# Four-layer residual kernel on one core: four buffers of lags with their folded half built on the core, x1 loaded ahead of the adapter stack, and weights laid out by the host

## The reference

```python
x = x + _L0_cond_ref(x, itok_B_8_3872, ...)   # long convolution per channel
x = x + _L1_cond_ref(x, itok_B_0_15, ...)     # 64x64 channel mix, chosen per sample
x = x + _L2_cond_ref(x, itok_B_6_15, ...)     # x W2^T + bias + rank-16 adapter, chosen per sample
x = x + _L3_cond_ref(x, itok_B_0_2, ...)      # x W3^T + rank-32 adapter, chosen per sample
```

## Time and profile before

| | us |
|---|---|
| median of three runs | 1584.57 |
| the profiled execution | 1583.27 |
| its span, first to last instruction | 1581.1 |
| PE busy | 1487.6 (94%) |
| DVE busy | 1073.5 (68%) |
| ACT busy | 635.6 (40%) |
| POOL busy | 116.0 (7%) |

### The profile page before, as it was taken

The page is one execution under the profiler, slowest core; times in us unless marked ns, Lnnn a source line. Parts: engine busy times, 40 slices in busy tenths (PEclk is TensorE's granted clock), DMA queues, the critical chain, the costliest instruction groups (busy, mean ns, idle before and its releaser), DMA issues.

```text
span 1581.1 us, 33465 instructions
## 1 busy us (share of the span) xinstructions
PE 1487.6 (94%) x10701; PEld 1422.1 (90%) x10701; DVE 1073.5 (68%) x2203; ACT 635.6 (40%) x1185; POOL 116.0 (7%) x197
## 2 busy tenths in 40 slices
PE   6999999999999996999999999999999999999998
PEld 5888888999989895999999999999999999999988
DVE  7955376676766674676676776677677677677674
ACT  3331256565666652243243243233243233333332
POOL 3551210000000000000000000000000000000000
PEclk9999999999999996999999999999999999999999
DMA  9724289899999986345445445545545545545642
GB/s 244 108 103 114 46 254 294 280 291 298 291 292 286 295 255 209 126 147 178 154 146 180 153 145 174 160 127 185 163 126 186 153 138 162 177 139 159 180 140 74
DMA packets 183699, 289.73 MB, mean 183 GB/s; under 512 B 64065, under 2 KB 120781, under 8 KB 181009
## 3 DMA queue, kind: packets, MB, share of 16 engines
q1 hardware_dynamic: 173436, 254.72, 53.8%
q10 hardware_dynamic: 10230, 34.59, 6.4%
HBM read 214.09 MB, written 75.15 MB: 183 GB/s over the span
## 4 chain that ended last, share of the span: by engine, by line
PE 34%; DMA 9%; SPq 9%; issue 6%; DVE 4%; DVEq 0%; ACT 0%
PE ps L1554 11%; PE ps L1555 11%; DMA x_in<-x_d 8%; PE ps L1525 6%; SPq L1223 5%; SPq L1222 3%; DVE late L1385 2%; PE ps L1564 2%; PE ps L1562 2%; PE ps L1536 1%; PE ps L1531 1%; DVE hrow L1444 1%; DVE hrow L1440 1%; DMA x_nat<-in_x 0%; DVE x_in L1390 0%
## 5 line engine op out<-in xcount | busy, mean ns | idle before, releaser
L1554 PE MATMUL ps<-weights,xs 128*128 128x256 f32 x1536 | 397.4, 289 | 0.0
L1555 PE MATMUL ps<-weights,xs 128*128 128x256 f32 (+1 forms) x1536 | 388.9, 292 | 0.0
L1554 PE MATMUL ps<-weights,xa 128*128 128x352 f32 (+1 forms) x1152 | 331.5, 315 | 4.4 <-DVE weights L1416 1.3
L1555 PE MATMUL ps<-weights,xa 128*128 128x256 f32 (+1 forms) x1152 | 325.5, 297 | 0.0
L1554 PEld LDWEIGHTS ps<-weights,xs 128*128 128x128 f32 x1536 | 292.6, 190 | 0.0
L1555 PEld LDWEIGHTS ps<-weights,xs 128*128 128x128 f32 x1536 | 292.5, 190 | 0.0
L1304 ACT ACTIVATE a<-ps 128x512 f32<-128x512 f32 x128 | 76.6, 599 | 396.6 <-PE ps L1525 396.6
L1554 PEld LDWEIGHTS ps<-weights,xa 128*128 128x128 f32 x1152 | 220.6, 192 | 9.6 <-issue 9.6
L1097 PE MATMUL ps<-toep,ut 128*128 128x512 f32 (+2 forms) x1152 | 227.6, 342 | 0.0
L1555 PEld LDWEIGHTS ps<-weights,xa 128*128 128x128 f32 x1152 | 219.2, 190 | 0.0
L1097 PEld LDWEIGHTS ps<-toep,ut 128*128 128x128 f32 x1152 | 195.0, 189 | 16.8
(11 more groups left out here) (221 smaller groups left out, 2095.6 us busy)
## 6 DMA issues: line engine op xcount, KB each, us to landing
xt<-in_xt SPq DMA_DIRECT2D x64, 512.0 KB, 6.8
x_d<-yo SPq DMA_DIRECT2D x64, 512.0 KB, 4.0
x_in<-x_d SPq DMA_DIRECT2D x64, 512.0 KB, 4.8
x_nat<-in_x SPq DMA_DIRECT2D x64, 512.0 KB, 3.9
out<-y_out ACTq DMA_DIRECT2D x64, 512.0 KB, 4.3
toep_raw<-kern_d SPq DMA_DIRECT2D x64, 384.0 KB, 5.0
toep_raw<-fold_d SPq DMA_DIRECT2D x64, 320.0 KB, 6.3
stack<-b_d SPq DMA_DIRECT2D x130, 128.0 KB, 3.6
```

Source lines behind the costliest of these rows:

```text
L1554: mm(left[0], x_part, left[1], start=first and is_wide, stop=end, skip_group_check=True)
L1555: ins = mm(right[0], x_part, right[1], start=first and is_wide and H_AT[m] > 0, stop=end, skip_group_check=True)
```

## The change

The change has four parts.

1. **Lags.** SP loads one piece of 1024 lags a channel (`lags`, four buffers) instead of 768 plain and 640 folded ones (two buffers). The folded part is no longer made once for all channels in DRAM: DVE adds it up in each channel from `lags` into `fold` (`sums`), two channels ahead, together with the difference of quarters. `fold_in`, `fold_sum` and `fold_d` are gone. `toep` is then rounded in two instructions on ACT and two on DVE instead of one each. `ut` is rounded for seven of its eight blocks (`SPLIT`). The block `tri` is copied behind `dt`, not before it. `yo` has two buffers instead of four, and `lags` and `xt` are both loaded three channels ahead. Before the loop SP waits until the last adapter rows are stored.
2. **Order of loads in a pair.** `load_stack` for pair n moves from the end of round n-1 to round n, behind the loads of `x1_in` for n+1. It reads its adapter numbers again (four `TENSOR_LOAD` more a round).
3. **Mask.** `late` has 16-bit elements and half the columns; its halves and tiles now share one buffer, so a mask waits for the copy before it (`chosen`).
4. **Layout by the host.** W2, W3 and the adapter factors arrive so that what a partition loads is one run in DRAM; 25 loads of factors become 4.

The diff, cut to its core:

```diff
 
             def load_p2(to, i, landed):
-                cols = slice(i * P, (i + 1) * P)
-                sp.dma_start(to[:], w2.rearrange("(c p) t -> p c t", p=P)[:, :, cols]).then_inc(landed, 16)
+                sp.dma_start(to[:], w2[i]).then_inc(landed, 16)
...
-                sp.dma_start(a3raw[:, c, :].rearrange("p (l r) -> p l r", r=R3),
-                             lora3_a.rearrange("l (c p) r -> c p l r", p=P)[c]).then_inc(in_a3, 16)
-            b2_in = lora2_b.rearrange("a (c p) r -> c p a r", p=P)
-            split = 3 * P // R2
-            for c in range(K8):
-                sp.dma_start(b2raw[:, c, :].rearrange("p (a r) -> p a r", r=R2), b2_in[c, :, 0:split]).then_inc(in_b2, 16)
-            for c in range(K8):
-                sp.dma_start(b2raw3[:, c, :].rearrange("p (a r) -> p a r", r=R2), b2_in[c, :, split:A2N]).then_inc(in_b2_3, 16)
-            sp.dma_start(b3_raw[:], lora3_b.rearrange("(c p) r -> p c r", p=P)).then_inc(in_b3, 16)
+            sp.dma_start(a3raw[:], lora3_a).then_inc(in_a3, 16)
+            sp.dma_start(b2raw[:], lora2_b[:, :, 0:3 * P]).then_inc(in_b2, 16)
+            sp.dma_start(b2raw3[:], lora2_b[:, :, 3 * P:AR]).then_inc(in_b2_3, 16)
+            sp.dma_start(b3_raw[:], lora3_b).then_inc(in_b3, 16)
...
 
-            def load_toep(k, u):
+            def load_lags(k, u):
                 h = UNROLL * k + u
-                ready(sp, toep_hi, h - 1)
-                ready(sp, toep_lo, h - 1)
-                raw, landed = toep_raw[u % 2], toep_in[u % 2]
-                sp.dma_start(raw[:, TFOLD:], toep_view[bass.ds(h, 1), :, :].squeeze(0)).then_inc(landed, 16)
-                sp.dma_start(raw[:, 0:TFOLD], fold_view[bass.ds(h, 1), :, :].squeeze(0)).then_inc(landed, 16)
+                ready(sp, tri_ready, h - BUFS + 1)
+                ready(sp, toep_lo, h - BUFS + 1)
+                sp.dma_start(lags[u % BUFS][:], toep_view[bass.ds(h, 1), :, :].squeeze(0)).then_inc(lags_in[u % BUFS], 16)
 
             def store_y(k, u):
                 sp.wait_ge(y_front, UNROLL * k + u + 1)
                 sp.wait_ge(y_back, UNROLL * k + u + 1)
-                sp.dma_start(x1_d[:, bass.ds(UNROLL * k + u, 1), :].squeeze(1), yo[u % BUFS][:]).then_inc(x1_stored[u % BUFS], 16)
-
-            sp.wait_ge(fold_stored, 16)
+                sp.dma_start(x1_d[:, bass.ds(UNROLL * k + u, 1), :].squeeze(1), yo[u % 2][:]).then_inc(x1_stored[u % 2], 16)
+
+            sp.wait_ge(kern_stored, 32)
             sp.wait_ge(staged_lo, len(STAGED))
-            load_toep(0, 0)
+            load_lags(0, 0)
             load_x(0, 0)
             for half in range(2):
                 sp.dma_start(mix[C * half:C * half + C], mix_w.rearrange("s c d -> c s d")).then_inc(in_mix, 16)
             sp.wait_ge(p3_part, 1)
             load_x(0, 1)
             sp.wait_ge(job_done, JOBS)
-            load_toep(0, 1)
+            load_lags(0, 1)
+            load_lags(0, 2)
             load_x(0, 2)
             sp.wait_ge(job_free, freed("b2_3"))
             sp.dma_start(b2_rows[3 * P:4 * P], f(b2_last[:])).then_inc(b2_stored, 16)
+            sp.wait_ge(b2_stored, 16 * (AR // P))
 
             def channel(k, u, loads=True):
 
-                if loads or u < UNROLL - 2:
-                    load_toep(k + (u + 2) // UNROLL, (u + 2) % UNROLL)
                 if loads or u < UNROLL - AHEAD:
+                    load_lags(k + (u + AHEAD) // UNROLL, (u + AHEAD) % UNROLL)
                     load_x(k + (u + AHEAD) // UNROLL, (u + AHEAD) % UNROLL)
                 store_y(k, u)
 
...
 
             def split_high(k, u):
                 h = UNROLL * k + u
-                act.wait_ge(x_in[u % BUFS], x_count(k, u) + 16)
+                act.wait_ge(x_in[u % BUFS], count_in(k, u) + 16)
                 ready(act, conv_done, h - 1)
-                copy(ut[u % 2][:, 0], xt[u % BUFS][:], ACT.Copy).then_inc(ut_hi, 1)
-                act.wait_ge(toep_in[u % 2], toep_count(k, u) + 32)
-                copy(toep[u % 2][:, 0], toep_raw[u % 2][:, ::-1], ACT.Copy).then_inc(toep_hi, 1)
-                copy(tri[u % 2][:], toep_raw[u % 2][:, :TOEP + TFOLD - P - 1:-1], ACT.Copy).then_inc(tri_ready, 1)
+                copy(ut[u % 2][:, 0, 0:SPLIT], xt[u % BUFS][:, 0:SPLIT], ACT.Copy).then_inc(ut_hi, 1)
+                act.wait_ge(lags_in[u % BUFS], count_in(k, u) + 16)
+                copy(toep[u % 2][:, 0, 0:TOEP], lags[u % BUFS][:, :T - TOEP - 1:-1], ACT.Copy)
+                act.wait_ge(fold_ready, h + 1)
+                copy(toep[u % 2][:, 0, TOEP:], fold[:, ::-1], ACT.Copy).then_inc(toep_hi, 1)
                 act.wait_ge(diff_ready, h + 1)
                 copy(dt[u % 2][:, 0], udiff[:], ACT.Copy).then_inc(dt_hi, 1)
+                copy(tri[u % 2][:], lags[u % BUFS][:, :T - P - 1:-1], ACT.Copy).then_inc(tri_ready, 1)
 
             def front(k, u):
...
+            def sums(k, u):
+
+                dve.wait_ge(lags_in[u % BUFS], count_in(k, u) + 16)
+                ready(dve, toep_lo, UNROLL * k + u)
+                tt(fold[:], lags[u % BUFS][:, 0:TFOLD], lags[u % BUFS][:, QT:QT + TFOLD], ALU.add).then_inc(fold_ready, 1)
+                dve.wait_ge(x_in[u % BUFS], count_in(k, u) + 16)
+                ready(dve, dt_lo, UNROLL * k + u)
+                raw = xt[u % BUFS]
+                tt(udiff[:], raw[:, 0:2], raw[:, 2:4], ALU.subtract).then_inc(diff_ready, 1)
+
             def split_low(k, u):
                 h = UNROLL * k + u
-                dve.wait_ge(x_in[u % BUFS], x_count(k, u) + 16)
-                ready(dve, dt_lo, h)
-                raw = xt[u % BUFS]
-                tt(udiff[:], raw[:, 0:2], raw[:, 2:4], ALU.subtract).then_inc(diff_ready, 1)
                 dve.wait_ge(ut_hi, h + 1)
-                tt(ut[u % 2][:, 1], raw[:], f(ut[u % 2][:, 0]), ALU.subtract).then_inc(ut_lo, 1)
+                tt(ut[u % 2][:, 1, 0:SPLIT], xt[u % BUFS][:, 0:SPLIT], f(ut[u % 2][:, 0, 0:SPLIT]), ALU.subtract).then_inc(ut_lo, 1)
                 dve.wait_ge(toep_hi, h + 1)
-                tt(toep[u % 2][:, 1], toep_raw[u % 2][:, ::-1], f(toep[u % 2][:, 0]), ALU.subtract).then_inc(toep_lo, 1)
+                tt(toep[u % 2][:, 1, 0:TOEP], lags[u % BUFS][:, :T - TOEP - 1:-1], f(toep[u % 2][:, 0, 0:TOEP]), ALU.subtract)
+                dve.wait_ge(fold_ready, h + 1)
+                tt(toep[u % 2][:, 1, TOEP:], fold[:, ::-1], f(toep[u % 2][:, 0, TOEP:]), ALU.subtract).then_inc(toep_lo, 1)
                 dve.wait_ge(dt_hi, h + 1)
                 tt(dt[u % 2][:, 1], udiff[:], f(dt[u % 2][:, 0]), ALU.subtract).then_inc(dt_lo, 1)
 
             def back(k, u):
 
                 h = UNROLL * k + u
-                y, to = ps[2 + u % 2], yo[u % BUFS]
+                y, to = ps[2 + u % 2], yo[u % 2]
                 dve.wait_ge(conv_done, h + 1)
                 dve.wait_ge(y_front, h + 1)
                 tt(to[:, HB:HB + QT], y[:, HB:HB + QT], shared_in[:], ALU.add)
                 tt(to[:, HB + QT:T], y[:, HB + QT:T], shared_in[:], ALU.subtract).then_inc(y_back, 1)
 
-            def channel(k, u, ahead=True):
-                if ahead:
+            def channel(k, u, ahead=2):
+                if ahead > 0:
                     split_low(k + (u + 1) // UNROLL, (u + 1) % UNROLL)
+                if ahead > 1:
+                    sums(k + (u + 2) // UNROLL, (u + 2) % UNROLL)
                 back(k, u)
 
             dve.wait_ge(p3_part, 1)
+            sums(0, 0)
             split_low(0, 0)
             b2_low(3, b2_last)
+            sums(0, 1)
             for u in range(UNROLL):
                 channel(0, u)
             with dve.Fori(1, GROUPS - 1) as k:
                 for u in range(UNROLL):
                     channel(k, u)
             for u in range(UNROLL):
-                channel(GROUPS - 1, u, ahead=u < UNROLL - 1)
+                channel(GROUPS - 1, u, ahead=UNROLL - 1 - u)
 
         @block.tensor
         def _(pe):
...
@@ -1240,12 +1227,22 @@
                 sp.wait_ge(chosen[v], 2)
                 load_x(1, v)
 
+            def stacks(n):
+
+                if isinstance(n, int) and n == 0:
+                    return
+                sp.wait_ge(p_done, n)
+                for v in range(2):
+                    load_stack(v, ids(sp, n, v, B))
+
             def pair(n, last_one):
+                sp.wait_ge(mixed, 4 * n + 4)
                 if last_one:
+                    stacks(n)
                     return
-                sp.wait_ge(mixed, 4 * n + 4)
                 for v in range(2):
                     load_x1(n + 1, v)
+                stacks(n)
                 a, l = [ids(sp, n + 1, v, B) for v in range(2)], [ids(sp, n + 1, v, 2 * B) for v in range(2)]
                 for v in range(2):
                     sp.wait_ge(h_lo[v], n + 1)
@@ -1257,9 +1254,6 @@
                     for v in range(2):
                         sp.wait_ge(chosen[v], 2 * n + 4)
                         load_x(n + 2, v)
-                sp.wait_ge(p_done, n + 1)
-                for v in range(2):
```

(23 more changed lines are left out.)

85 lines of the change are left out of this document (34 added, 51 removed).

## The result

The changed kernel took 1518.57 us (median of 4 runs, 1517.08 to 1523.25) against 1583.78 us before (4 runs, 1578.46 to 1592.93): a ratio of 0.9588, with a 95% interval from 0.9538 to 0.9637. The forecast was 1527, its range 1517 to 1547. The profiled run took 1518.57 us for a span of 1516.8, 64.3 less than the 1581.1 of before.

What follows compares the result with a forecast made beforehand. PE bounds the kernel except where it waits: for DVE's row sums in the pairs, for transfers in the convolution. 1583.3 - 40 - 17 + 0.7 = 1527.0 us, range 1517 to 1547.

Steps and rivals of the forecast that it cites:

- -40: Pairs: `x_in` issued earlier ends PE's waits at the turn of v = 0; 40 us less, bounds 36.3 and 43.7.
- -17: Convolution: fewer bytes a channel nearly end ACT's wait for lags, PE becomes the bound; 17 us less, bounds 0 and 21.8.
- the transfers set the pace wherever PE does not: Convolution: 1728 KB a channel at 286 GB/s need 6.19 us, over PE's 5.76; the new 1536 KB need 5.50.
- 4.7 us were forecast: Convolution: DVE's new load per channel, 5.4 of 5.76 us with two hand-offs from ACT; fits with little room.
- +0.7: Start of the convolution: DVE's longer chain before channel 0, with the added sum, costs 0.7 us more.
- The set-up loads: Set-up: PE does not wait for the loads of W2 and factors; W3's strips give 0 to -4.4 us, taken as 0.
- The rival of 1523: Set-up: the new layout also ends the waits for W3, giving 1523 us; chance 0.07.
- The mask: Pairs: halves sharing a buffer wait 0.15 to 0.3 us four times in a pair; cost to the time nothing.
- SP's queue: Pairs: four more reads add 2.8 us, last table issued at 1028.7 instead of 1025.22; cost nothing, with 1.1 us of cover.
- even sharing: Pairs: four 512 KB transfers share the engines evenly, all end after 7.3 us, 1.3 too late; sum 1566.
- the rule: Pairs: engines alternate between queues by packets, so the output's first store ends with the first load; wait near 0.4, sum 1527.
- The fourth rival: Pairs: the output's store lands so late that ACT's copy holds up M2; slower, 1602 us at 8.5 us; chance 0.04.

Runs made afterwards that it cites:

- the run with three sums: The changed kernel with DVE's sum of the folded lags made three times in each channel: 1557.16 us, ratio 0.9815 to before.
- the kernel with copies: The changed kernel with two 512 KB DRAM-to-DRAM copies more in each pair, issued behind `x_in`: 1540.99 us, ratio 0.9717 to before.

## Why the prediction was right

**The pairs: right, undersized.** The term was -40, between 36.3 and 43.7; the stage lost 44.5, and the order alone gave the period of the whole. The term was mis-sized where it took the middle of its two bounds. From the first turn of v = 0 to the 31st, 30 pairs, are 898.6 us before (635.8 to 1534.4) and 853.9 after (616.4 to 1470.3). These 44.7 us are the whole of what the stage lost, and 1.0 above 43.7, the idle time before the weight load with the restart in it. The idle time before the matmul, 36.3, was too small a measure.

**The convolution: right in size, wrong in a step.** The term was -17 of at most 21.8; the stage lost 20.4. The 4.8 us kept back for the first channel and for turns of the loop were too many: behind the first channel PE never stood still. The step that failed is "the transfers set the pace wherever PE does not", with its 1728 KB at 286 GB/s. The same bytes move under PE at 308 GB/s with the load issued a channel earlier, and fewer bytes without that bring half. The way from issue to use, which the forecast named as a help ("8.8 us now from issue to first need"), was what held the old loop, and the circle has the bytes work only through the length of a transfer. For a changed kernel that moved the 1728 KB, the forecast's reason would have said that nothing is gained; the run with 192 KB more shows all but 2.8 us of the stage gained, and nothing lost in the time. Whether issuing earlier would do it alone, in the kernel before, no run shows.

**DVE: right in load, wrong in room.** 4.7 us were forecast and 4.7 come out of the run with three sums. The hand-offs did not belong in the sum: DVE had 1.06 us free in a channel and not 0.36.

**The start of the convolution and the set-up.** +0.7 and 0 were forecast; the set-up ended 0.9 later. PE's wait for channel 0 is 2.61 us for 2.68, so the longer chain of DVE did not show there: that the sum, +0.9, came near +0.7 is luck. Kernels with one and the same set-up differ by up to 2.6 us at this point, so one trace can't size a term of 0.7. That such a chain can count is shown by the kernels with more sums, which wait there for 3.39 us (two) and 4.12 us (three); what made up for the first sum stays open.

**The set-up loads: right.** Nothing, in 10 runs of the layout alone (0.9973 to 1.0012). The rival of 1523 falls.

**The mask: right.** Nothing, measured side by side with the changed kernel.

**SP's queue: right, on a thin cover.** The tables left 0.95 us later than worked out. That is small by luck, for two errors nearly cancel: the four new reads took 5.7 us (4.23 and 1.49) and not 2.8, and the eight `stack` loads 3.6 and not 5.6. Why the first two reads are slow stays open. In the kernel before, eight reads behind the same two loads took 5.5 us, so the loads alone do not do it. The waits for tables were absorbed by DVE and ACT; with 0.95 us more of queue, in the kernel with copies, they no longer were.

**The late store.** By even sharing the store would have taken 7.3 us and cost 39; by the rule it would have stayed near 4.0. It took 5.36, between the two, and M2 did not wait, so the time came out as with the rule, with 0.6 us of the 2.0 left over. The Trainium skill, page DMA: Bandwidth & Descriptors, section Queues, rings and completion order, has the engines take turns between queues and keep the order within one. Two more transfers behind `x_in` left the first store's wait at 1.55 us, which agrees with it. The 1.4 us more do not come from `x_in` alone. In the kernel with the order alone the store meets the same transfers, and its buffer comes free after 4.01 us:

```profile
1023.34 0.37 ACTq L1368 DMA_DIRECT2D out<-y_out  x1
...
1027.35 0.60 ACT L1346 ACTIVATE y_out<-ps 128x512 f32<-128x512 f32 x1 [0.43 <-DMA out<-y_out]
```

Over the pairs ACT's mean wait for this store is 0.45 us before (11.7 / 26), 0.78 there (21.7 / 28) and 1.55 in the changed kernel. So the order moved it by 0.3 us, near the rule's nothing, and some other part of the change by 0.8 more. The mask is not that part (42.4 / 28 with 8 bits); which one it is was not tried. The fourth rival's "no transfer of this size in the earlier trace rows takes over 6.8" misread the rows: these are medians, and `xt` took up to 8.0 us there.

Together: 4.5 us from the pairs, 3.4 from the convolution and 0.3 between the stages, less 0.2 at the set-up, are 8.0 of the 8.4 by which 1527.0 was above 1518.57; the other 0.4 lies around the span (2.2 us before, 1.8 now).

## What to carry to other kernels

A rate read from a stage that waits is what the loop asked for, not what the engines can give: before you divide bytes by it, add up the circle from the event that lets the load be issued to the use of its data, and compare it with the number of iterations it may take. Hand-off waits of an engine that runs ahead are slack, so compare its start-to-start load alone with the bound. In a queue written out by hand, put first the load whose reader is the next to hold up the bound; then check what the reordering made last, here the tables, because that is where the next change will pay.
